# The maxima's rows of two score units added by four 32-row products instead of four 64-row ones

## The chip, the cores and the metric

The kernel runs on one core of one Trainium2 chip, as one launch. The metric is the device time of that launch in microseconds. A core has TensorE for matrix products (PE in the profile, its weight loads PEld), VectorE (DVE), ScalarE (ACT), GpSimd (POOL) and a queue that issues transfers (SP). The engines run side by side and wait for each other only at semaphores. TensorE writes to PSUM, eight banks of 512 float columns on 128 partitions, which VectorE and ScalarE can read.

## The reference, cut to what matters

The program is a chain of four layers on 1024 tokens and 6404 context rows of width 128: a slot attention, a causal attention with experts, a Perceiver cross attention, and a dense mixture of experts. The change lies in the third, which is this, for 16 heads of 64 columns:

```python
x = layer_norm(x, ln1_w, ln1_b)                 # 6404 context rows
lat = layer_norm(latents, ln2_w, ln2_b)         # 1024 latents
lat = lat * (1.0 + scale[:, None, :]) + shift[:, None, :]
q = jnp.einsum('bld,ed->ble', lat, Wq)
kv_in = jnp.concatenate((x, lat), axis=-2)      # 7428 keys
kv = jnp.einsum('bld,ed->ble', kv_in, Wkv)
...
logits = jnp.einsum('bhqd,bhkd->bhqk', q * attn_scale, k * attn_scale)
w = jax.nn.softmax(logits.astype(jnp.float32), axis=-1).astype(logits.dtype)
out = jnp.einsum('bhqk,bhkd->bhqd', w, v)
```

Every query has its own largest logit over 7428 keys, and the softmax subtracts it before the exponential.

## The kernel before

The work is cut into 16 halves `h`: two heads (one on partitions 0 to 63, the other on 64 to 127) and 512 of the 1024 queries. Within a half the keys come in 15 steps `s` of 512 keys, each of four units `i` of 128 keys; the last step (`s = 14`) has the units 56, 57 and 58, the last with four keys only. The names below are those of the code.

A unit (`scores`, L1917 on) makes the scores of 128 keys by 512 queries for both heads, in a slot of two PSUM banks. There are two slots, taken in turn, so a unit waits (`wait_free`) until ScalarE has read the unit two before it. Per head four products of 64 rows add up in one bank: `m = 0` adds the negated maxima, by a matrix with ones in the head's first row (`one_rows`) against `q_shift`, which holds the negated maxima in that row; `m = 1, 2, 3` are the parts of a product in two precisions (`k_high` with `q_high`, `k_low` with `q_high`, `k_high` with `q_low`). The products of the two heads use different rows of the array and run side by side. ScalarE then takes the exponential of both banks in one instruction (L2021) and writes `probs`.

Between these products stand the fills (L1913): plain 64-row products for the maxima of the next half. Each goes to one of three banks (`fill_bank`), VectorE reduces it (L2070), and a fill waits (`peaked`) until all reductions up to that of the third fill before it are done. Every unit of the halves 0 to 14 has one fill per head, placed among its products by `PLACES`; in a step's first unit it stands ahead of them, with place `(0, 0)`. In the last step one more pair of fills stands ahead of the first unit. Half 15 has no fills.

After a step's four units TensorE does, in odd halves, a `produce` (keys and values of the next pair of heads, L1891 and L1897), and then the adds (L1954): eight products of 128 rows by 64 columns that weigh the values with the previous step's `probs`. The order of all this is one list (`perceiver_order`), and every engine walks through it.

The maxima of a half are reduced (L2110) and negated (L2112) into `peak` on VectorE, transposed on TensorE (`shift`, L1962) and copied to `q_shift` by ScalarE. `one_rows` and `peak` are cleared by VectorE in a block of its own ahead of the layer (L1826 on).

Of the kernel before, what the change touches and what calls it, by code (L numbers as in the profile page):

```python
# [4 lines left out]
F32 = mybir.dt.float32  # L5


F32R = mybir.dt.float32r
# [1650 lines left out]

PLACES = ((0, 0), (0, 1), (0, 0), (0, 2))  # L1660


def turns_of(place):

    lanes = [[(head, m) for m in range(4)] for head in range(2)]
    for head in range(2):
        lanes[head].insert(place[head], ("fill", head))
    return [turn for both in zip(*lanes) for turn in both]
# [72 lines left out]
def perceiver_attention(k, A, rows):  # L1741
# [16 lines left out]
    values_of = {e[3:5]: n for e, n in made_values.items()}  # L1758
    scored = {e[1:3]: number[e] for e in entries if e[0] == "scores"}
    fills = []  # L1760
    for e in order:
# [7 lines left out]
    with ExitStack() as ctx:  # L1769
# [5 lines left out]
        q_shift = k.sb("pair_q_shift", [P, HALF], F32R, ctx=ctx)  # L1775
        one_rows = k.sb("pair_one_rows", [P, P], F32R, ctx=ctx)
        probs = k.sb("pair_probs", [P, 2, 4, 2, HALF], ctx=ctx)
        total = k.sb("pair_total", [P, 2, HALF], ctx=ctx)
# [12 lines left out]
        heads = (slice(0, HD1), slice(HD1, P))  # L1791
        peak_columns = peak[:].rearrange("p (n c) -> p n c", c=TQ)[:, 0:HD1 // TQ + 1:HD1 // TQ, :]

        def wait(engine, name, n):
            if n > 0:
                engine.wait_ge(S[name].sem, S[name].at(n))
# [28 lines left out]
        with nc.Block() as block:  # L1825
            @block.vector  # L1826
            def _(v):
                v.memset(one_rows[:].bitcast(F32), 0.0).then_inc(S["cleared"].sem, 1)
                v.memset(peak[:], 0.0).then_inc(S["cleared"].sem, 1)
                wait(v, "cleared", 2)  # L1830
                for row in (0, HD1):
                    v.memset(one_rows[row:row + 1].bitcast(F32), 1.0).then_inc(S["cleared"].sem, 1)
                wait(v, "cleared", 4)

        with nc.Block() as block:
# [21 lines left out]
            def _(pe):  # L1857
# [43 lines left out]
                def fill(f, head):  # L1901
# [8 lines left out]
                    else:  # L1910
# [4 lines left out]
                              stop=True).then_inc(S["filled"].sem, 1)  # L1915

                def scores(e, h, i, f):  # L1917
                    wait_free(e)
                    if i == 0:
                        wait(pe, "qlow", number["queries", h])  # L1920
                        wait(pe, "shifted", number["shift", h])
                    if i % 4 == 0:
                        wait(pe, "low", keys_of[h // 2, i // 4])
                    n = parts_of(i)
                    r, columns = ring_of(h // 2, i // 4), slice(i % 4 * P, i % 4 * P + n)
# [6 lines left out]

                    turns = [(head, m) for m in range(4) for head in range(2)]
                    if f is not None:
                        turns = turns_of(PLACES[i % 4])
                    final = [turn for turn in turns if turn[0] != "fill"][-1]
# [21 lines left out]
                def shift(e, h):  # L1958
                    wait_free(e)
                    wait(pe, "negated", number["peak", h])  # L1960
                    for t in range(TQ):
                        last = pe.transpose(slot(e)[:, 0, t * P:(t + 1) * P], peak[:, t:t + P], k.ident[:])  # L1962
                    last.then_inc(S["made"].sem, 1)
# [94 lines left out]
            def _(v):  # L2058
# [28 lines left out]
                for e in order:  # L2087
# [17 lines left out]
                    elif e[0] == "peak":  # L2105
                        h = e[1]
                        wait(v, "peaked", 2 * fill_number["fill", h, LAST, TQ - 1] + 2)
                        if h:
                            wait_made(v, ("shift", h - 1))
                        v.reduce_max(peak_columns, peaks[:], axis=AX).then_inc(S["largest"].sem, 1)  # L2110
                        wait(v, "largest", h + 1)
                        v.tensor_scalar(peak_columns, peak_columns, -1.0, None, ALU.mult).then_inc(S["negated"].sem, 1)  # L2112
                    elif e[0] == "sum":
# [141 lines left out]
```

## Time and profile before

| | us |
|---|---|
| median of 3 runs | 3549.62 |
| lowest and highest | 3545.74 and 3551.71 |
| the profiled execution's own time | 3550.18 |
| its span in the trace | 3548.5 |

| engine | busy us | share of the span |
|---|---|---|
| PE | 3184.4 | 90% |
| DVE | 2474.4 | 70% |
| POOL | 1872.4 | 53% |
| PEld | 1860.8 | 52% |
| ACT | 1690.0 | 48% |

The span is that of the instructions on the chip, and the execution's own time lies 1.7 us above it. The Perceiver layer takes the part from some 1014 us to 3400 us. An entry of the timeline has the start, the length, the engine and the line, what is written and read, the shape of the tile of weights (`64*128` is 64 rows by 128 columns), the number of instructions merged, and in brackets the idle time before it with its releaser. Matmuls are pipelined: the distance of two starts says how long the first one holds the array, and the length of an entry is longer than that.

### The profile page before, as it was taken

The numbers are of one execution on the slowest core, as the hardware profiler recorded it, in microseconds if no ns is written. First come the engines' busy times: TensorE is split into PE (matmuls) and PEld (weight loads), VectorE is DVE, ScalarE is ACT, GpSimd is POOL, SyncE is SP. The second block draws the span as 40 slices with busy tenths as digits, with TensorE's granted clock in tenths as the row PEclk, the third lists the DMA queues.
The fourth block names the chain that finished last, engine by engine and source line by source line (L and its number), as shares of the span: only waits on it lengthen the run. The fifth ranks groups of instructions, "written<-read, shape, count | busy, mean of one in ns | idle before, by whom it ended". The sixth has DMA issues, their size and how long they took to land. (4 is left out here: it accounts for less than half of the span.)

```text
span 3548.5 us, 51026 instructions
## 1 busy us (share of the span) xinstructions
PE 3184.4 (90%) x18472; PEld 1860.8 (52%) x18472; DVE 2474.4 (70%) x4297; ACT 1690.0 (48%) x2048; POOL 1872.4 (53%) x1158
## 2 busy tenths in 40 slices
PE   5979797586448999999999999999999999999977
PEld 3757575332324555555555555555555555555435
DVE  6979797653258776877777777687777777768431
ACT  5758585243213444454444444445444444444432
POOL 3857575111222655655655565565565566556750
PEclk8989898566679999999999999999999999999988
DMA  1000000000410000000000000000000000000000
GB/s 62 1 1 1 1 1 1 12 1 1 139 21 3 1 1 1 4 1 1 4 1 1 1 4 1 1 4 1 1 4 1 1 1 2 1 1 1 1 26 7
DMA packets 20416, 28.21 MB, mean 8 GB/s; under 512 B 5064, under 2 KB 12368, under 8 KB 20048
## 3 DMA queue, kind: packets, MB, share of 16 engines
q1 hardware_dynamic: 18832, 21.83, 1.9%
q0 software_dynamic: 1344, 3.15, 0.3%
q8 instruction: 154, 2.52, 0.3%
q14 instruction: 86, 0.70, 0.1%
HBM read 21.30 MB, written 3.67 MB: 7 GB/s over the span
## 5 line engine op out<-in xcount | busy, mean ns | idle before, releaser
L2021 ACT ACTIVATE pair_probs<-banks 128x1024 f32<-128x1024 f32 (+1 forms) x944 | 965.7, 1026 | 1035.8 <-PE banks L1931 983.9
L2070 DVE TENSOR_REDUCE pair_peaks<-banks 128x1 f32<-128x512 f32 (+1 forms) x1800 | 1086.4, 666 | 271.3 <-PE banks L1913 257.9
L2163 POOL TENSOR_TENSOR pair_total_pool<-pair_total_pool,pair_probs 128x1536 f32<-128x1536 f32 x208 | 724.5, 3483 | 754.2 <-DVE pair_total L2084 749.0
L1954 PE MATMUL banks<-pair_probs,pair_values 128*64 128x512 f32 (+1 forms) x3776 | 872.9, 600 | 0.0
L1913 PE MATMUL banks<-pair_k_high,pair_q_high 64*128 64x512 f32 (+1 forms) x1920 | 567.3, 442 | 27.3 <-DVE pair_peaks L2063 14.8
L2152 POOL TENSOR_TENSOR pair_total_pool<-pair_total_pool,pair_probs 128x1024 f32<-128x1024 f32 x224 | 536.0, 2393 | 39.1 <-POOL pair_total_pool L2163 21.5
L2084 DVE TENSOR_TENSOR pair_total<-pair_total,pair_probs 128x512 f32<-128x512 f32 (+2 forms) x464 | 458.2, 988 | 94.3 <-ACT pair_probs L2021 69.1
L1954 PEld LDWEIGHTS banks<-pair_probs,pair_values 128*64 128x64 f32 (+1 forms) x3776 | 248.3, 136 | 472.8 <-issue 384.9
L1931 PE MATMUL banks<-pair_q_shift,pair_one_rows 64*128 64x512 f32 (+1 forms) x1888 | 476.1, 396 | 3.1 <-ACT pair_probs L2021 3.1
L1913 PEld LDWEIGHTS banks<-pair_k_high,pair_q_high 64*128 64x128 f32 x1920 | 262.8, 184 | 356.1 <-issue 212.3
L1931 PE MATMUL banks<-pair_q_high,pair_k_high 64*128 64x512 f32 (+1 forms) x1888 | 427.5, 391 | 0.0
L1931 PE MATMUL banks<-pair_q_low,pair_k_high 64*128 64x512 f32 (+1 forms) x1888 | 381.3, 390 | 0.0
L1931 PE MATMUL banks<-pair_q_high,pair_k_low 64*128 64x512 f32 (+1 forms) x1888 | 380.8, 390 | 0.0
L1931 PEld LDWEIGHTS banks<-pair_q_shift,pair_one_rows 64*128 64x128 f32 (+1 forms) x1888 | 243.7, 184 | 34.3 <-ACT pair_probs L2021 11.5
L766 POOL TENSOR_TENSOR value_tile<-context_rows,slot_small 128x128 f32<-128x128 f32 x153 | 198.3, 1296 | 88.4 <-DVE slot_small L638 84.4
L1931 PEld LDWEIGHTS banks<-pair_q_high,pair_k_high 64*128 64x128 f32 (+1 forms) x1888 | 221.8, 183 | 33.7
L2098 DVE TENSOR_TENSOR pair_k_low<-banks,pair_k_high 128x512 fp32r<-128x512 f32 (+1 forms) x120 | 80.9, 674 | 220.5 <-ACT pair_k_high L2031 219.3
L543 ACT ACTIVATE slot_probs<-banks,slot_small 128x1024 f32<-128x1024 f32 x153 | 171.1, 1118 | 81.9 <-DVE slot_small L645 81.9
L1931 PEld LDWEIGHTS banks<-pair_q_high,pair_k_low 64*128 64x128 f32 (+1 forms) x1888 | 184.4, 183 | 40.0 <-issue 0.8
L1931 PEld LDWEIGHTS banks<-pair_q_low,pair_k_high 64*128 64x128 f32 (+1 forms) x1888 | 184.9, 183 | 38.3
L643 DVE TENSOR_REDUCE slot_small<-banks 128x1 f32<-128x1024 f32 x153 | 187.0, 1222 | 19.1 <-PE banks L439 7.7
L651 DVE TENSOR_TENSOR slot_probs_low<-slot_probs,slot_probs_high 128x1024 fp32r<-128x1024 f32 x153 | 193.0, 1261 | 6.3 <-ACT slot_probs_high L547 5.5
(325 smaller groups left out, 3776.3 us busy)
## 6 DMA issues: line engine op xcount, KB each, us to landing
expert_w<-in_fc SPq DMA_DIRECT2D x32, 256.0 KB, 3.6
context_rows<-in_ctx SPq DMA_DIRECT2D x10, 320.0 KB, 6.7
dense_w<-in_We SPq DMA_DIRECT2D x2, 1024.0 KB
experts_in<-expert_zeros SPq DMA_DIRECT2D x1, 1024.0 KB, 3.8
expert_b<-in_fc_b SPq DMA_DIRECT2D x2, 512.0 KB, 5.0
expert_rows<-experts_in SPq DMA_DIRECT2D x16, 64.0 KB, 1.9
experts_out<-expert_result POOLq DMA_DIRECT2D x4, 256.0 KB, 3.7
row_parameters<-in_rows SPq DMA_DIRECT2D x1, 896.0 KB, 8.7
```

Of the source, the lines that this page charges most:

```text
L543: done("expd", act.activation(probs[0:n, r, :], flat(scores[r][0:n]), ACT.Exp, bias=small[0:n, r, 1:2], scale=SLOT_SCALE, accum_out=small[ ...
L643: done("largest", v.reduce_max(small[0:n, r, 0:1], flat(scores[r][0:n]), axis=AX))
L651: done("subbed", v.tensor_tensor(probs_low[0:n, r, 0:TOKENS], probs[0:n, r, 0:TOKENS], probs_high[0:n, r, 0:TOKENS].bitcast(F32), ALU.subt ...
L766: done("weighed", pool.tensor_tensor(value[0:n, r, :], rows[0:n, i, :], small[0:n, r, 3:4].to_broadcast([n, D]), ALU.mult))
L1913: pe.matmul(bank[:, 0:width(b)], q_high[h % 2][heads[head], t * P:(t + 1) * P], k_high[heads[head], ring_of(h // 2, b), 0:width(b)], start ...
L1931: return pe.matmul(slot(e)[0:n, head, :], left, right, start=m == 0, stop=m == 3)
L1954: last = pe.matmul(out[heads[head], :], values[0:n, ring_of(h // 2, i // 4), i % 4, heads[head]], probs_of(h, i)[0:n, head, :], start=i == ...
L2021: act.activation(probs_of(h, i)[0:n], slot(e)[0:n], ACT.Exp, scale=1.0 / 8.0).then_inc(S["expd"].sem, 1)
L2070: v.reduce_max(peaks[:, head, t, b:b + 1], fill_bank(f, head)[:, 0:width(b)], axis=AX).then_inc(S["peaked"].sem, 1)
L2084: v.tensor_tensor(total[0:n, both], total[0:n, both], probs_of(h, i)[0:n, both], ALU.add).then_inc(S["summed"].sem, 1)
L2152: pool.tensor_tensor(pooled[:, 1:3], pooled[:, 1:3], probs_of(h, 4 * s + 3), ALU.add).then_inc(S["pooled"].sem, 1)
L2163: pool.tensor_tensor(pooled[:], pooled[:], three, ALU.add).then_inc(S["pooled"].sem, 1)
```

## The change

In a step, the first two units are a pair if both stand next to each other in the list of slots, in one step, and no `output` or `denominators` stands just before them. That gives 210 pairs: 15 in half 0 and 13 in each of the others.

Where a pair starts, TensorE waits for both slots and then issues four products of 32 rows (`share_shift`), one for each head of each unit, into four banks. `q_shift` now holds the negated maxima in rows 0, 32, 64 and 96, and `lane_rows` has ones in these rows. The two units then make their products `m = 1, 2, 3` alone. All other units keep their own `m = 0` with `one_rows`. The maxima are first reduced to a tile of their own (`largest`) and then negated into two places of `peak`, by two instructions. The number of TensorE's products stays the same.

```diff
 PLACES = ((0, 0), (0, 1), (0, 0), (0, 2))
+LANE = 32
+FIRST_OF_TWO = (0,)
-def turns_of(place):
-    lanes = [[(head, m) for m in range(4)] for head in range(2)]
+def turns_of(products, place):
+    lanes = [[(head, m) for m in products] for head in range(2)]
     for head in range(2):
-        lanes[head].insert(place[head], ("fill", head))
+        if place is not None:
+            lanes[head].insert(place[head], ("fill", head))
...
+    partner = {}
+    for n, e in enumerate(entries[:-1]):
+        if e[0] == "scores" and e[2] % 4 in FIRST_OF_TWO and entries[n + 1][0:2] == e[0:2] and e[2] < TILES \
+                and entries[n + 1][2] // 4 == e[2] // 4 and entries[n - 1][0] not in ("output", "denominators"):
+            partner[e] = entries[n + 1]
+    second = set(partner.values())
...
-                wait(v, "cleared", 2)
+                v.memset(lane_rows[:].bitcast(F32), 0.0).then_inc(S["cleared"].sem, 1)
+                wait(v, "cleared", 3)
                 for row in (0, HD1):
                     v.memset(one_rows[row:row + 1].bitcast(F32), 1.0).then_inc(S["cleared"].sem, 1)
-                wait(v, "cleared", 4)
+                for row in range(0, P, LANE):
+                    v.memset(lane_rows[row:row + 1].bitcast(F32), 1.0).then_inc(S["cleared"].sem, 1)
+                wait(v, "cleared", 9)
...
+                def share_shift(units):
+                    for u, unit in enumerate(units):
+                        n = parts_of(unit[2])
+                        for head in range(2):
+                            lane = slice(head * HD1 + u * LANE, head * HD1 + (u + 1) * LANE)
+                            pe.matmul(slot(unit)[0:n, head, :], lane_rows[lane, 0:n], q_shift[lane, :], start=True, stop=False)
+
                 def scores(e, h, i, f):
-                    wait_free(e)
+                    if e not in second:
+                        wait_free(e)
...
+                    if e in partner:
+                        wait_free(partner[e])
+                        share_shift((e, partner[e]))
...
-                    turns = [(head, m) for m in range(4) for head in range(2)]
-                    if f is not None:
-                        turns = turns_of(PLACES[i % 4])
+                    products = range(1, 4) if e in partner or e in second else range(4)
+                    turns = turns_of(products, None if f is None else PLACES[i % 4])
...
-                    wait(pe, "negated", number["peak", h])
+                    wait(pe, "negated", 2 * number["peak", h])
...
-                        v.reduce_max(peak_columns, peaks[:], axis=AX).then_inc(S["largest"].sem, 1)
+                        v.reduce_max(largest[:], peaks[:], axis=AX).then_inc(S["largest"].sem, 1)
                         wait(v, "largest", h + 1)
-                        v.tensor_scalar(peak_columns, peak_columns, -1.0, None, ALU.mult).then_inc(S["negated"].sem, 1)
+                        for columns in peak_columns:
+                            v.tensor_scalar(columns, largest[:], -1.0, None, ALU.mult).then_inc(S["negated"].sem, 1)
```

How the instructions move is shown by TensorE's list at a step's start, from a unit's last product to the third unit. The shapes in these lists are those of the result. In the kernel before, L1954 is an add, L1913 a fill, and L1931 the products of a unit, `pair_q_shift` being `m = 0`:

```order
3909 L1954 MATMUL banks<-pair_probs,pair_values 64x512 x8
3910 L1913 MATMUL banks<-pair_k_high,pair_q_high 128x512 x2
3911 L1931 MATMUL banks<-pair_q_shift,pair_one_rows 128x512 x2
3912 L1931 MATMUL banks<-pair_q_high,pair_k_high 128x512 x2
3913 L1931 MATMUL banks<-pair_q_high,pair_k_low 128x512 x2
3914 L1931 MATMUL banks<-pair_q_low,pair_k_high 128x512 x2
3915 L1913 MATMUL banks<-pair_k_high,pair_q_high 128x512
3916 L1931 MATMUL banks<-pair_q_shift,pair_one_rows 128x512 x2
3917 L1913 MATMUL banks<-pair_k_high,pair_q_high 128x512
3918 L1931 MATMUL banks<-pair_q_high,pair_k_high 128x512 x2
```

The same place in the changed kernel, where the lines are L1979 for the add, L1928 for the fill, L1957 for a unit's products, and L1937 for the shared ones:

```order
3851 L1979 MATMUL banks<-pair_probs,pair_values 64x512 x8
3852 L1937 MATMUL banks<-pair_q_shift,pair_lane_rows 128x512 x4
3853 L1928 MATMUL banks<-pair_k_high,pair_q_high 128x512 x2
3854 L1957 MATMUL banks<-pair_q_high,pair_k_high 128x512 x2
3855 L1957 MATMUL banks<-pair_q_high,pair_k_low 128x512 x2
3856 L1957 MATMUL banks<-pair_q_low,pair_k_high 128x512 x2
3857 L1928 MATMUL banks<-pair_k_high,pair_q_high 128x512
3858 L1957 MATMUL banks<-pair_q_high,pair_k_high 128x512 x2
3859 L1928 MATMUL banks<-pair_k_high,pair_q_high 128x512
3860 L1957 MATMUL banks<-pair_q_high,pair_k_low 128x512 x2
```

The four shared products stand between the adds and the first unit's fills. The first unit has as many turns ahead of its last product as before, and the second unit has one turn fewer.

In a half's last step TensorE's list reads so in the kernel before, with the extra pair of fills and the first unit's pair in one row:

```order
2932 L1954 MATMUL banks<-pair_probs,pair_values 64x512 x8
2933 L1913 MATMUL banks<-pair_k_high,pair_q_high 128x260 x4
2934 L1931 MATMUL banks<-pair_q_shift,pair_one_rows 128x512 x2
2935 L1931 MATMUL banks<-pair_q_high,pair_k_high 128x512 x2
2936 L1931 MATMUL banks<-pair_q_high,pair_k_low 128x512 x2
```

And so in the changed one, at the same kind of place:

```order
4997 L1979 MATMUL banks<-pair_probs,pair_values 64x512 x8
4998 L1928 MATMUL banks<-pair_k_high,pair_q_high 128x260 x2
4999 L1937 MATMUL banks<-pair_q_shift,pair_lane_rows 128x512 x4
5000 L1928 MATMUL banks<-pair_k_high,pair_q_high 128x260 x2
5001 L1957 MATMUL banks<-pair_q_high,pair_k_high 128x512 x2
5002 L1957 MATMUL banks<-pair_q_high,pair_k_low 128x512 x2
```

Here the shared products come between the two pairs of fills. 15 of the 210 pairs are of this kind, and 13, those of half 15, have no fills at all.

## Rows read from the trace of the kernel before

**Rows 1.** The page: busy time by engine, and the granted clock in 40 slices.
```profile
PE 3184.4 (90%) x18472; PEld 1860.8 (52%) x18472; DVE 2474.4 (70%) x4297; ACT 1690.0 (48%) x2048; POOL 1872.4 (53%) x1158
...
PEclk8989898566679999999999999999999999999988
```
**Rows 2.** Stretch of the layer: window, length, busy of PE, PEld, DVE, ACT, POOL, PEclk.
```profile
1500.00:2000.00 500.00, 496.44 (x3092) 271.59 (x3090) 367.40 (x555) 241.92 (x273) 290.11 (x108) 1.00 0.01 2
```
**Rows 3.** Timeline of PE in one step of half 2: start, length, instruction.
```profile
1489.34 0.50 PE L1913 MATMUL banks<-pair_k_high,pair_q_high 64*128 64x512 f32 x2
1489.67 0.39 PE L1931 MATMUL banks<-pair_q_shift,pair_one_rows 64*128 64x512 f32 x2
1489.90 0.39 PE L1931 MATMUL banks<-pair_q_high,pair_k_high 64*128 64x512 f32 x2
...
1490.37 0.39 PE L1931 MATMUL banks<-pair_q_low,pair_k_high 64*128 64x512 f32 x2
...
1491.52 0.41 PE L1931 MATMUL banks<-pair_q_low,pair_k_high 64*128 64x512 f32 x2
1491.88 0.50 PE L1913 MATMUL banks<-pair_k_high,pair_q_high 64*128 64x512 f32 x2
```
**Rows 4.** Timeline of PEld in the same step, where its third unit starts.
```profile
1491.88 0.19 PEld L1913 LDWEIGHTS banks<-pair_k_high,pair_q_high 64*128 64x128 f32 x2 [0.38 <-ACT pair_probs L2021]
1491.99 0.19 PEld L1931 LDWEIGHTS banks<-pair_q_shift,pair_one_rows 64*128 64x128 f32 x2
```
**Rows 5.** Timeline of ACT in that step, its first and second exponential.
```profile
1490.80 1.03 ACT L2021 ACTIVATE pair_probs<-banks 128x1024 f32<-128x1024 f32 x1 [3.91 <-PE banks L1931]
...
1491.96 1.03 ACT L2021 ACTIVATE pair_probs<-banks 128x1024 f32<-128x1024 f32 x1
```
**Rows 6.** Timeline of DVE in that step, its first and third reduction.
```profile
1489.87 0.69 DVE L2070 TENSOR_REDUCE pair_peaks<-banks 128x1 f32<-128x512 f32 x1 [1.69 <-PE banks L1913]
...
1491.08 0.68 DVE L2070 TENSOR_REDUCE pair_peaks<-banks 128x1 f32<-128x512 f32 x1
```
**Rows 7.** Waits of PEld, 1100 to 3400 us: total, times, longest.
```profile
PEld banks L1913 <- ACT pair_probs L2021: 111.3, 359, 0.5
```
**Rows 8.** Timeline of PE: from 64-row products to 128-row ones.
```profile
1494.08 0.39 PE L1931 MATMUL banks<-pair_q_low,pair_k_high 64*128 64x512 f32 x2
1494.40 1.08 PE L1954 MATMUL banks<-pair_probs,pair_values 128*64 128x512 f32 x4
```
**Rows 9.** Timelines of PEld and PE: adds of 128 rows, then of 4.
```profile
1247.68 0.17 PEld L1954 LDWEIGHTS banks<-pair_probs,pair_values 128*64 128x64 f32 x2 [0.26 <-issue]
1248.11 0.17 PEld L1954 LDWEIGHTS banks<-pair_probs,pair_values 128*64 128x64 f32 x2 [0.26 <-issue]
...
1248.57 1.17 PE L1954 MATMUL banks<-pair_probs,pair_values 128*64 128x512 f32 x3
...
1249.09 1.07 PE L1954 MATMUL banks<-pair_probs,pair_values 4*64 4x512 f32 x4
```
**Rows 10.** Timelines in the causal layer: four 32-column tiles, two 25-row tiles.
```profile
703.61 0.20 PEld L1013 LDWEIGHTS banks<-causal_probs,values_by_head 128*32 128x32 f32 x4 [0.44 <-issue]
...
700.24 0.79 PE L994 MATMUL banks<-keys,queries 25*128 25x512 f32 x2 [0.69 <-ACT causal_probs L1103]
```
**Rows 11.** Timeline of PE in a step of half 15, without fills.
```profile
3388.59 0.50 PE L1931 MATMUL banks<-pair_q_shift,pair_one_rows 64*128 64x512 f32 x2
...
3390.91 0.50 PE L1931 MATMUL banks<-pair_q_shift,pair_one_rows 64*128 64x512 f32 x2 [0.20 <-ACT pair_probs L2021]
```
**Rows 12.** Timelines of PE and DVE in the last step of half 2.
```profile
1523.94 0.50 PE L1913 MATMUL banks<-pair_k_high,pair_q_high 64*128 64x260 f32 x3
1524.84 0.39 PE L1913 MATMUL banks<-pair_k_high,pair_q_high 64*128 64x260 f32 x1 [0.40 <-DVE pair_peaks L2070]
...
1525.18 0.52 PE L1931 MATMUL banks<-pair_q_high,pair_k_high 64*128 64x512 f32 x2
...
1524.36 0.43 DVE L2070 TENSOR_REDUCE pair_peaks<-banks 128x1 f32<-128x260 f32 x1 [1.58 <-PE banks L1913]
```
**Rows 13.** Timelines of DVE: the rows of ones, and the negation in half 0.
```profile
1015.32 0.41 DVE L1832 MEMSET pair_one_rows<- 1x128 f32 x2
...
1104.91 0.17 DVE L2112 TENSOR_SCALAR pair_peak_columns<-pair_peak_columns 128x8 f32<-128x8 f32 x1
```

More of the change, by code:

```diff
@@ L1776, in perceiver_attention @@
         one_rows = k.sb("pair_one_rows", [P, P], F32R, ctx=ctx)
+        lane_rows = k.sb("pair_lane_rows", [P, P], F32R, ctx=ctx)
+        largest = k.sb("pair_largest", [P, 2, TQ], ctx=ctx)
         probs = k.sb("pair_probs", [P, 2, 4, 2, HALF], ctx=ctx)
@@ L1791, in perceiver_attention @@
         heads = (slice(0, HD1), slice(HD1, P))
-        peak_columns = peak[:].rearrange("p (n c) -> p n c", c=TQ)[:, 0:HD1 // TQ + 1:HD1 // TQ, :]
+        peak_columns = [peak[:].rearrange("p (n c) -> p n c", c=TQ)[:, lane // TQ:(lane + HD1) // TQ + 1:HD1 // TQ, :]
+                        for lane in (0, LANE)]
         def wait(engine, name, n):
```

## Prediction

> **What bounds the kernel now.** I read the page's busy times and clock first, then the windows of the layer, then the timelines of one step on PE, PEld, ACT and DVE, and last what ended the idle times. TensorE is busy 90% of the span, and its granted clock is at the full level of 2.4 GHz from the middle of the slices on [rows 1]; within the layer it is busy 496.44 of 500 us [rows 2]. By that share each product saved would count. The reader is to distrust this: an entry of a matmul is longer than the distance to the next one, so a stall of a tenth of a microsecond is covered by it.
>
> One step shows the stall. The pair of fills starts at 1489.34 and the first product pair at 1489.67, 0.33 later; the next follows at 1489.90, 0.23 later [rows 3]. So a pair of 64-row products holds the array for 0.23, and the first after a pause costs 0.10 to 0.11 more, which is its weights' load: at 1491.88 and 1491.99 the loads of two pairs start 0.11 apart [rows 4]. The first unit's last pair starts at 1490.37 [rows 3]; its exponential runs from 1490.80 for 1.03 us, to 1491.83 [rows 5]; the third unit, which needs the first one's slot, starts at 1491.88 [rows 3], with ACT named as the releaser and its loads idle for 0.38 [rows 4]. The second unit's last pair had started at 1491.52 [rows 3], so TensorE would have been ready at 1491.75: it waits 0.13 there. The chain from the step's start to its third unit is thus first unit, exponential, third unit: 1.03 + 0.43 + 1.03 + 0.05 = 2.54 us. The second unit lies beside it. The same wait stands in the whole layer: 359 idle times of the fills' loads end by ACT, 0.31 us each [rows 7], where halves 0 to 14 have 225 steps. Half 15, without fills, waits there too, 0.20 us of PE's own idle time [rows 11].
>
> A second chain runs close beside it. VectorE starts the first fill's reduction at 1489.87 and the third at 1491.08, which ends at 1491.76 [rows 6]: three reductions back to back, 0.60 apart. The second fill of the third unit goes to a bank which the third of these reductions must have left. With a hand-over of 0.05 it could go at 1491.81, and goes at 1491.88 [rows 3]. So this chain has 0.07 us to spare. The hand-over from VectorE is seen in the last step: a reduction from 1524.36 for 0.43 us, to 1524.79, and the waiting fill at 1524.84 [rows 12].
>
> **The change part by part.** I count from a step's start, t = 0.
>
> The four shared products take the array once, 0.23, in place of two pairs, 2 x 0.23. The second of these was the second unit's, which lies beside the chain through the exponential. What it frees, 210 x 0.23 = 48 us, comes ahead of a stall that nothing shortens: the exponential of the first unit still follows that unit's last product, with just as many turns ahead of it as before. The gain on the path is zero.
>
> What is added is on the path. The array goes from 32-row products back to 64-row ones right behind the shared four. The rows show what a change of the rows costs. From a 64-row pair to 128-row adds it takes 0.32 instead of 0.23 (1494.08 to 1494.40) [rows 8]. Between adds, which follow each other at 0.43 (1247.68, 1248.11), the change from 128 rows to 4 takes 0.52 (1248.57 to 1249.09) [rows 9]. Each is 0.09 over the usual distance, and then the new weights' load is exposed as after a pause, another 0.11 for 128 columns. The change from the adds into the first scores was there before, so only one is new. I put the first unit's fills at 0.11 + 0.23 + 0.09 = 0.43 instead of 0, its `m = 1` at 0.43 + 0.34 = 0.77 instead of 0.57, and its last product 0.20 later than now. No row has 32 rows followed by 64, so the bounds are 0 (the loads are pulled ahead as between 64-row pairs) and 0.20; I take 0.20, since both row-count changes that the trace has cost it.
>
> The Trainium skill says in "TensorEngine Tiling (Array Packing)", Key Properties, that a change of the tiling mode drains TensorE, while a change of the tile within a mode doesn't. By this rule 64 to 32 to 64 rows is two changes and each waits for the array; rows 8 and 9 agree in size, 0.09 us. Without such a drain the fills would come at 0.34 and the first unit's last product not later at all.
>
> By the chain over ScalarE alone the third unit comes 0.20 later. By the chain over VectorE it is worse: the first fill, and with it the first reduction, moves by 0.43, while the reductions stay 0.60 apart. The third ends at 2.42 + 0.43 = 2.85, and the third unit's second fill can go at 2.90 instead of 2.54: 0.36 later. That is the larger one and sets the end. TensorE issues in order, so behind this fill stand the third unit's own products, its exponential, the fourth unit and the adds. Afterwards nothing gives the time back: fourth unit and adds run at TensorE's pace.
>
> Of the 210 pairs 13 are in half 15, with no fills: 13 x 0.20 = 2.6 us. 15 are in last steps, where an extra pair of 260-column fills comes first. There the first unit's second fill already waits for VectorE until 1524.84, 0.90 after the step's start, and its `m = 1` starts at 1525.18, or 1.24 [rows 12]. The shared four now fit into that wait: extra fills 0.11 + 0.11, drain 0.09, the four and the way back 0.43, so 0.74, still under 0.90; then `m = 1` comes at 0.90 + 0.11 + 0.11 = 1.12. That is 0.1 earlier: 15 x 0.1 = 1.5 us gained. The other 182 give 182 x 0.36 = 65.5 us.
>
> Small edits: one more clearing of a tile and four more rows of ones, in a block that the layer waits for. Two rows of ones take 0.41 with the second 0.24 behind the first [rows 13], so four add 1.0, and the tile some 0.15: 1.1 us once. The second negation is exposed in half 0 alone, where TensorE waits for it: 0.17 to 0.25, taken as 0.2 [rows 13]. In other halves adds stand between. The wait for the second slot at a pair's start costs nothing as long as the four adds, 8 x 0.43 = 3.4 us, cover the last exponential (0.43 + 1.03 + 0.05 behind the fourth unit's last product). In odd halves the copies of keys and values are in that slot; they have the same 3.4 us. Without this cover each such step would lose what is missing. For the wait's own instruction I take nothing; TensorE's queue reads it while the adds run.
>
> Sum: 65.5 + 2.6 - 1.5 + 1.1 + 0.2 = 67.9 us. Against the profiled execution, 3550.18, that is 3618.1. The median of the runs is 0.6 lower, which gives 3617.5; I say 3617.
>
> **The rivals.**
>
> *The way back to 64 rows is free.* Then the fills come at 0.34, `m = 1` where it is now, and ScalarE's chain is unchanged. VectorE's chain still shifts: 2.42 + 0.34 + 0.05 = 2.81 against 2.54, 0.27 for 182 pairs, or 49 us; with 1.3 for the small edits and 1 or 2 off in last steps, 3599. For it: pairs in different halves of the array overlap their loads already. Against it: rows 8 and 9.
>
> *Only ScalarE's chain counts.* The reductions turn out to have more room, say because they could start closer together once fills wait for them. Then 182 x 0.20 + 2.6 - 1.5 + 1.3 = 38.8, so 3588. Against it: three reductions run back to back now.
>
> *The four products don't run wholly side by side.* At the worst they go two by two, 0.23 more: the fills at 0.66, VectorE's chain at 0.59, ScalarE's at 0.43: 182 x 0.59 + 13 x 0.43 + 1 + 1.3 = 115, so 3665. The rows have four loads merged in 0.20 us for 32-column tiles, and two 25-row tiles at once [rows 10], but never four row tiles; the lower bound is nothing, and I take the four as one.
>
> The Trainium skill gives in "TensorE: Matmul & The Clock Gate", Measured speedup vs the span model, 3.07 times for four tiles of 32 rows by 512 columns. Four over 3.07 is 1.30 of one product, an estimate of 0.07 us more each; the sum would be 182 x 0.43 + 13 x 0.27 and the same small terms, some 82 us, so 3631. No row here shows it.
>
> *Faster: the turn saved counts.* If TensorE and not the exponential set the start of the third unit, and changes of rows were free, 210 x 0.23 = 48 us would go: 3501. It decides from the point where the exponential of the first unit ends before the second unit's last turn is over; now it ends 0.08 after it. For it speak only the busy shares of rows 1 and 2; against it rows 4, 7 and 11.
>
> *No change.* The way back is free and VectorE keeps up after all: 3551.
>
> **How the numbers follow.** Forecast 0.58, free way back 0.12, ScalarE alone 0.08, four products wider 0.13 (spread between 3625 and 3665), no change 0.04, faster 0.05. The range from 3582 to 3645 holds the first three and about half of the fourth, 0.84 in all; inside the forecast a drain of 0.05 to 0.12 and a hand-over of 0.05 to 0.15 give 3609 to 3640. About 0.2%, 7 us, is what a measurement of this kernel can tell from no change. Faster 0.05, within it 0.04, slower 0.91.
>
> **What would show it.** In the new timeline the distance from the shared four to the fills should be 0.43, from a step's first product to its third unit 2.90 for the second fill and some 2.74 for the first, with VectorE as the releaser of the second; a step should be 0.36 longer in halves 1 to 14, and 0.20 in half 15. VectorE's first reduction should start 0.96 after the step's start instead of 0.53. The distance 0.34 would show the free way back; two loads of the shared four 0.2 apart would show that they don't overlap; and idle loads of the third unit named after ACT alone would show that VectorE's chain doesn't count. It is wrong altogether if the third unit starts less than 2.5 us after the step.

## The result, and the profile after

The changed kernel takes 3610.2 us (median of 4 runs, 3607.47 to 3612.32), the kernel before 3549.05 (4 runs, 3545.74 to 3551.71). The ratio is 1.0172, with a 95% interval of 1.0155 to 1.019: slower by 61 us, where 67.9 were forecast (3617, range 3582 to 3645). A turn, here as in the prediction, is one pair of products side by side, 0.23 us of the array. The profiled execution has 3610.98 us and a span of 3609.3.

The page again shows a TensorE that is 90% busy, and not where the loss is. Both its busy time and the span grew, by 48 and 61 us:

```profile
PE 3232.2 (90%) x18472; PEld 1944.7 (54%) x18472; DVE 2459.3 (68%) x4318; ACT 1687.6 (47%) x2048; POOL 1869.0 (52%) x1158
...
PEclk8989898666779999999999999999999999999988
```

The timeline of PE for a full step of half 2 and the start of the next (start, length, instruction) answers to [rows 3]:

```profile
1512.04 0.50 PE L1937 MATMUL banks<-pair_q_shift,pair_lane_rows 32*128 32x512 f32 x4
...
1521.02 0.50 PE L1937 MATMUL banks<-pair_q_shift,pair_lane_rows 32*128 32x512 f32 x4
1521.45 0.50 PE L1928 MATMUL banks<-pair_k_high,pair_q_high 64*128 64x512 f32 x2
1521.78 0.39 PE L1957 MATMUL banks<-pair_q_high,pair_k_high 64*128 64x512 f32 x2
...
1522.23 0.39 PE L1957 MATMUL banks<-pair_q_low,pair_k_high 64*128 64x512 f32 x2
...
1523.74 0.68 PE L1928 MATMUL banks<-pair_k_high,pair_q_high 64*128 64x512 f32 x2
```

From the shared four to the fills it is 0.43, as forecast, and to `m = 1` 0.76 (forecast 0.77). The first unit's last product is 1.21 after the step's start, where it was 1.03. The third unit's first fill is 2.72 after it; before it was 2.54. The entry of the pair of fills at 1523.74 is 0.68 long instead of 0.50: its two halves don't start together any more. A step takes 1521.02 - 1512.04 = 8.98. In the kernel before the same stretch took 8.65:

```profile
1480.69 0.50 PE L1913 MATMUL banks<-pair_k_high,pair_q_high 64*128 64x512 f32 x2
```

(the next step there starts at 1489.34 [rows 3]).

The timelines of ACT and DVE in that step, first exponential, then first and third reduction:

```profile
1522.66 1.03 ACT L2046 ACTIVATE pair_probs<-banks 128x1024 f32<-128x1024 f32 x1 [4.10 <-PE banks L1957]
```
```profile
1521.98 0.69 DVE L2095 TENSOR_REDUCE pair_peaks<-banks 128x1 f32<-128x512 f32 x1 [2.17 <-PE banks L1928]
...
1523.18 0.68 DVE L2095 TENSOR_REDUCE pair_peaks<-banks 128x1 f32<-128x512 f32 x1
```

The first reduction starts 0.96 after the step's start (0.53 before [rows 6]) and the third ends at 1523.86. The loads of PEld around the third unit show when the second fill goes:

```profile
1523.74 0.36 PEld L1928 LDWEIGHTS banks<-pair_k_high,pair_q_high 64*128 64x128 f32 x2 [0.49 <-ACT pair_probs L2046]
1523.92 0.18 PEld L1957 LDWEIGHTS banks<-pair_q_shift,pair_one_rows 64*128 64x128 f32 x1
```

One load is 0.18; the pair's entry of 0.36 means that the second starts 0.18 after the first, at 1523.92: 2.90 after the step's start, 0.06 after the third reduction. That is the forecast number. The row's bracket names ACT, the releaser of the entry's first load; that the second one waits for VectorE is seen only from its start and the reduction's end. The 0.18 between the two loads is also just the length of one, so this step alone doesn't exclude that the second simply follows the first. The whole trace does: over the 181 steps that are like this one (regular steps, below), the second fill's load starts 0.053 to 0.054 after the end of the third reduction in nine tenths of them, while its distance to the first load varies from 0.15 to 0.18. In the kernel before it starts 0.12 to 0.14 after that reduction and 0.003 after the first load.

Half 15 has no fills, and a last step has an extra pair. Their PE rows answer to [rows 11, 12]:

```profile
3456.40 0.51 PE L1937 MATMUL banks<-pair_q_shift,pair_lane_rows 32*128 32x512 f32 x4
...
3458.91 0.50 PE L1957 MATMUL banks<-pair_q_shift,pair_one_rows 64*128 64x512 f32 x2 [0.42 <-ACT pair_probs L2046]
```
```profile
1538.96 0.39 PE L1928 MATMUL banks<-pair_k_high,pair_q_high 64*128 64x260 f32 x2
1539.28 0.51 PE L1937 MATMUL banks<-pair_q_shift,pair_lane_rows 32*128 32x512 f32 x4
1539.72 0.53 PE L1928 MATMUL banks<-pair_k_high,pair_q_high 64*128 64x260 f32 x2
1539.95 0.53 PE L1957 MATMUL banks<-pair_q_high,pair_k_high 64*128 64x512 f32 x2
```

In half 15 the third unit starts 2.51 after the step's start, 2.32 before [rows 11]. In the last step the first unit's `m = 1` comes 0.99 after the start instead of 1.24 [rows 12]: the shared four fit into the wait for VectorE.

To sum up the layer I took the time between the exponentials of the last units of successive steps, in the traces of both kernels. The 181 steps with a pair and fills (without last steps and the very first step; called regular steps below) are longer by 0.33 each, 59.9 us together. The 13 of half 15: 0.21 each, 2.7. The 15 last steps: shorter by 0.22, -3.3. The steps without a pair: -2.1, of which -2.4 in step 1 of the odd halves. There TensorE waits for GpSimd's sum, and a later arrival waits less. The very first step: -0.8. That is 56.4 us between the first and the last exponential, and 4.3 come before it. The waits of PE for that sum, before and then after (total, times, longest):

```profile
PE banks L1969 <- POOL pair_total_pool L2135: 5.5, 8, 0.7
```
```profile
PE banks L1994 <- POOL pair_total_pool L2161: 3.0, 8, 0.6
```

The eight waits, one in each odd half, are 2.5 us shorter in all.

### The profile page after: what moved, and what is told of

Read it like the earlier page. It is cut to its first block and busy times, and to the rows that moved or that the text cites. A ratio compares the mean times of both kernels' runs of the same rounds, so it can differ in the third digit from the quotient of the medians.

```text
span 3609.3 us, 50934 instructions
## 1 busy us (share of the span) xinstructions
PE 3232.2 (90%) x18472; PEld 1944.7 (54%) x18472; DVE 2459.3 (68%) x4318; ACT 1687.6 (47%) x2048; POOL 1869.0 (52%) x1158
## 5 line engine op out<-in xcount | busy, mean ns | idle before, releaser
L1979 PE MATMUL banks<-pair_probs,pair_values 128*64 128x512 f32 (+1 forms) x3776 | 873.0, 600 | 0.0
L1928 PE MATMUL banks<-pair_k_high,pair_q_high 64*128 64x512 f32 (+1 forms) x1920 | 618.2, 453 | 35.2 <-DVE pair_peaks L2088 14.2
L1979 PEld LDWEIGHTS banks<-pair_probs,pair_values 128*64 128x64 f32 (+1 forms) x3776 | 248.5, 136 | 472.1 <-issue 384.9
L1957 PE MATMUL banks<-pair_q_high,pair_k_high 64*128 64x512 f32 (+1 forms) x1888 | 464.6, 392 | 0.0
L1957 PE MATMUL banks<-pair_q_high,pair_k_low 64*128 64x512 f32 (+1 forms) x1888 | 457.9, 390 | 0.0
L1957 PE MATMUL banks<-pair_q_low,pair_k_high 64*128 64x512 f32 (+1 forms) x1888 | 457.5, 390 | 0.0
L1928 PEld LDWEIGHTS banks<-pair_k_high,pair_q_high 64*128 64x128 f32 x1920 | 292.7, 185 | 252.2 <-ACT pair_probs L2046 115.0
L1957 PEld LDWEIGHTS banks<-pair_q_low,pair_k_high 64*128 64x128 f32 (+1 forms) x1888 | 262.5, 183 | 16.5 <-issue 0.3
L1957 PEld LDWEIGHTS banks<-pair_q_high,pair_k_high 64*128 64x128 f32 (+1 forms) x1888 | 260.2, 183 | 15.6 <-issue 3.2
L1957 PEld LDWEIGHTS banks<-pair_q_high,pair_k_low 64*128 64x128 f32 (+1 forms) x1888 | 259.1, 183 | 15.5
L1957 PE MATMUL banks<-pair_q_shift,pair_one_rows 64*128 64x512 f32 (+1 forms) x1048 | 262.0, 394 | 5.9 <-ACT pair_probs L2046 5.9
L547 ACT ACTIVATE slot_probs_high<-slot_probs 128x1024 fp32r<-128x1024 f32 x153 | 162.3, 1061 | 5.4 <-PE banks L451 0.6
```

What stands on the lines that cost most here:

```text
L1928: pe.matmul(bank[:, 0:width(b)], q_high[h % 2][heads[head], t * P:(t + 1) * P], k_high[heads[head], ring_of(h // 2, b), 0:width(b)], start ...
L1957: return pe.matmul(slot(e)[0:n, head, :], left, right, start=m == 0, stop=m == 3)
L1979: last = pe.matmul(out[heads[head], :], values[0:n, ring_of(h // 2, i // 4), i % 4, heads[head]], probs_of(h, i)[0:n, head, :], start=i == ...
```

## The experiments

All are run beside the kernel before on the same chip, whose time is given with them. "Per step" is the mean change of the 181 regular steps, taken as above.

**e1_first_alone.** The row change without the saved turn.

```diff
-                    if e not in second:
-                        wait_free(e)
+                    wait_free(e)
...
                     if e in partner:
-                        wait_free(partner[e])
-                        share_shift((e, partner[e]))
+                        share_shift((e,))
...
-                    products = range(1, 4) if e in partner or e in second else range(4)
+                    products = range(1, 4) if e in partner else range(4)
```

> The changed kernel, but only the first unit's m = 0 goes through 32-row products (two of them, rows 0 and 64); the second unit keeps its own 64-row pair, so no turn is saved. Theory (the cost is the change of rows on the path of the first unit, the saved turn lies beside the stall and is worth nothing): the same as the changed kernel, 3610 within 5 us, and 0.33 us per step over before as there; the third unit's fills still start at 2.7 and 2.9 us after the step's start. Rival (the saved turns count, 210 x 0.23 us): 3658. Rival (four tiles hold the array longer than two): shorter than the changed kernel, by 0.05 us or more from the 32-row products to the fills.

Measured: 3616.87 us against 3553.18, ratio 1.0177 (1.0159 to 1.0194), which is the changed kernel's ratio; 0.345 per step. PE's timeline:

```profile
1503.68 0.50 PE L1937 MATMUL banks<-pair_q_shift,pair_lane_rows 32*128 32x512 f32 x2
1504.11 0.50 PE L1928 MATMUL banks<-pair_k_high,pair_q_high 64*128 64x512 f32 x2
...
1506.43 0.65 PE L1928 MATMUL banks<-pair_k_high,pair_q_high 64*128 64x512 f32 x2
```

The time itself lies 6.7 us above the changed kernel's 3610.2, a little more than the 5 allowed, but the kernel before was 4.1 us higher in these runs too; the ratios are the same. Giving the saved turn back costs nothing, or 0.01 per step. And two 32-row products take the same 0.43 to the fills as four: the four run side by side. Both rivals fall.

**e2_second_left_out.** The saved turn without the row change. On the changed kernel's source, without `share_shift`:

```diff
-                    if e in partner:
-                        wait_free(partner[e])
-                        share_shift((e, partner[e]))
...
-                    products = range(1, 4) if e in partner or e in second else range(4)
+                    products = range(1, 4) if e in second else range(4)
```

The first product that is left then starts the sum in the bank.

> The changed kernel without the shared products: the first unit of a pair has its own 64-row m = 0 as before, the second unit's m = 0 is left out (its maxima are not subtracted). This is the saved turn without the change of rows. Theory: worth nothing, since the second unit lies beside the first one's exponential: 3549 to 3552 us, steps as long as before, the third unit's wait longer by 0.23. Rival (TensorE is the bound, a turn is worth 0.23): 3549 - 48 = 3501.

Measured: 3551.68 us (10 runs) against 3553.18 (13), ratio 1.0 (0.999 to 1.0009); -0.015 per step. A step's start and its third unit on PE, and the third unit's loads:

```profile
1488.22 0.50 PE L1928 MATMUL banks<-pair_k_high,pair_q_high 64*128 64x512 f32 x2
...
1490.77 0.50 PE L1928 MATMUL banks<-pair_k_high,pair_q_high 64*128 64x512 f32 x2 [0.20 <-ACT pair_probs L2042]
```
```profile
1490.76 0.19 PEld L1928 LDWEIGHTS banks<-pair_k_high,pair_q_high 64*128 64x128 f32 x2 [0.63 <-ACT pair_probs L2042]
```

The third unit stands where it stood, 2.55 after the step's start, and its loads idle for 0.63 instead of 0.38 [rows 4]. 210 turns of 0.23 us, 48 us of TensorE's work, are gone and the time is the same. The rival of 3501 falls.

**e3_first_left_out.** A turn taken from the path of the first exponential. As e2, with the first unit's `m = 0` left out:

```diff
-                    products = range(1, 4) if e in partner or e in second else range(4)
+                    products = range(1, 4) if e in partner else range(4)
```

> As the last one, but the first unit's m = 0 of each pair is left out instead (its maxima are not subtracted), and the second unit has its own. Now a turn goes from the path of the exponential, while the first fills stay where they are. Theory of two chains: the exponential's chain gets shorter by 0.23 but VectorE's third reduction holds the third unit's second fill at 2.47 instead of 2.54, so 0.07 per step: 182 x 0.07 + 13 x 0.23 + 15 x 0.2 = 19 us, 3530, with VectorE as the releaser of the second fill. Rival (only ScalarE's chain counts): 210 x 0.23 = 48, 3501.

Measured: 3532.76 us against 3553.18, ratio 0.9945 (0.9929 to 0.9962). Per step -0.09 (expected -0.07), in half 15 -0.23, in last steps -0.23. The third unit on PEld in a step that starts at 1493.21, and VectorE's third reduction:

```profile
1495.53 0.34 PEld L1928 LDWEIGHTS banks<-pair_k_high,pair_q_high 64*128 64x128 f32 x2 [0.27 <-ACT pair_probs L2042]
```
```profile
1494.95 0.68 DVE L2091 TENSOR_REDUCE pair_peaks<-banks 128x1 f32<-128x512 f32 x1
```

The first fill goes at 2.32, the second 0.34 - 0.18 = 0.16 later, at 2.48, behind the reduction that ends at 2.42. Of 0.23 us that the exponential's chain gives back, 0.09 arrive; where there are no fills, all do. In nine tenths of the regular steps the second fill's load starts 0.052 to 0.054 after the third reduction, as in the changed kernel. VectorE's chain is the second bound, just under the first.

**e4_late_fill.** The changed kernel, with VectorE's chain out of the third unit's way:

```diff
-PLACES = ((0, 0), (0, 1), (0, 0), (0, 2))
+PLACES = ((0, 0), (0, 1), (0, 2), (0, 2))
```

> The changed kernel with the third unit's second fill two turns later (place 2 instead of 0 in PLACES), so that it does not wait for VectorE's third reduction. Theory: what is left is ScalarE's chain, 0.20 to 0.21 per step instead of 0.33, as in half 15: 3610 - 182 x 0.13 = 3586. Rival (VectorE's chain does not count, the 0.33 is all row changes): 3610. If VectorE is short of time later in the step, between the two.

Measured: 3585.57 us against 3553.18, ratio 1.0098 (1.0081 to 1.0115); 0.19 per step instead of 0.33. PE's timeline:

```profile
1496.68 0.50 PE L1937 MATMUL banks<-pair_q_shift,pair_lane_rows 32*128 32x512 f32 x4
...
1499.41 0.50 PE L1928 MATMUL banks<-pair_k_high,pair_q_high 64*128 64x512 f32 x1
1499.41 0.73 PE L1957 MATMUL banks<-pair_q_shift,pair_one_rows 64*128 64x512 f32 x2
```

Both halves of the array start at 2.73 now. This parts the loss in two: 0.19 to 0.20 by the row change through ScalarE, and 0.14 more by the late fills through VectorE. The kernel before was not run with this place, but the steps without a pair can stand in for that: in the 30 of them, of which 28 have fills, e4 and the changed kernel differ by 0.2 us in all. The move by itself is worth nothing there.

**e5_fills_first.** The changed kernel with the first unit's fills ahead of the shared four, so that VectorE starts early:

```diff
                     if e in partner:
                         wait_free(partner[e])
+                        if f is not None:
+                            for head in range(2):
+                                fill(f, head)
                         share_shift((e, partner[e]))
```

> The changed kernel with the first unit's fills ahead of the shared four instead of behind them, so the array goes 64 to 32 to 64 rows and VectorE's reductions start as early as before. Theory: two new changes of rows instead of one, so the first unit's m = 1 at 0.11 + 0.23 + 0.09 + 0.11 + 0.23 + 0.09 = 0.86 instead of 0.57, and the third unit 0.29 later, released by ScalarE alone; in last steps the shared four now stand behind the fill that waits for VectorE, so 0.4 lost instead of 0.22 gained. 182 x 0.29 + 15 x 0.4 + 2.7 - 2 = some 60 us over before: 3605 to 3615. Rival (the cost of the changed kernel is ScalarE's alone, one change of rows 0.33): 0.66 per step, 3670. Rival (changes of rows are free in themselves, the cost came from the late fills): 3550.

Measured: 3628.28 us against 3549.33, ratio 1.0219 (1.0203 to 1.0235). Per step 0.40, not 0.29; in last steps 0.41. This expectation missed by 0.11. PE's timeline:

```profile
1505.40 0.50 PE L1928 MATMUL banks<-pair_k_high,pair_q_high 64*128 64x512 f32 x2
1505.83 0.51 PE L1937 MATMUL banks<-pair_q_shift,pair_lane_rows 32*128 32x512 f32 x4
1506.27 0.51 PE L1960 MATMUL banks<-pair_q_high,pair_k_high 64*128 64x512 f32 x2
1506.61 0.40 PE L1960 MATMUL banks<-pair_q_high,pair_k_low 64*128 64x512 f32 x2
...
1508.37 0.50 PE L1928 MATMUL banks<-pair_k_high,pair_q_high 64*128 64x512 f32 x2 [0.19 <-ACT pair_probs L2049]
```

`m = 1` starts at 0.87, as worked out. But `m = 2` follows 0.34 later and not 0.23, since behind each change of rows the load is exposed; I had counted it for two of three. So a change of rows costs 0.20 each time, and two cost 0.40. The rest of the theory fits: the third unit starts 2.97 after the step's start, both fills at once and with ACT as the releaser, so the chain over ScalarE is the longer one and VectorE's early start gains nothing. Both rivals fall, 0.66 per step and no loss.

**e7_fills_ahead.** The kernel before, with the stall used. The third unit's fills don't need its slot, so they go ahead of the wait:

```diff
                 def scores(e, h, i, f):
+                    early = f is not None and i % 4 == 2
+                    if early:
+                        for head in range(2):
+                            fill(f, head)
                     wait_free(e)
...
-                    if f is not None:
+                    if f is not None and not early:
                         turns = turns_of(PLACES[i % 4])
```

> The kernel before (no shared products) with one move: the third unit's fills are issued ahead of the wait for its slot, since they need a bank of their own and not the slot. They fill the stall behind the first unit's exponential. Theory: the fills go at 2.41 and 2.47 (VectorE's third reduction ends at 2.42), the third unit's own products at 2.64 and 2.8 instead of 2.88, and the fourth unit waits for the second exponential until 3.70 instead of starting at 3.83: 0.13 us per step in 225 steps, 29 us, so 3520 (3512 to 3530). Rival (the stall moves whole to the fourth unit or to the adds): 3550. Rival (fills ahead collide with VectorE): slower than before.

Measured: 3544.19 us (11 runs) against 3549.33 (21), ratio 0.9988 (0.9979 to 0.9997); -0.03 per step, -0.24 in last steps. The expectation, 3520 and 0.13 per step, missed. PE's timeline of a step that starts at 1486.07, and the fourth unit's load:

```profile
1488.47 0.57 PE L1913 MATMUL banks<-pair_k_high,pair_q_high 64*128 64x512 f32 x2
1488.69 0.58 PE L1935 MATMUL banks<-pair_q_shift,pair_one_rows 64*128 64x512 f32 x2
...
1489.76 0.49 PE L1913 MATMUL banks<-pair_k_high,pair_q_high 64*128 64x512 f32 x1
```
```profile
1489.76 0.18 PEld L1913 LDWEIGHTS banks<-pair_k_high,pair_q_high 64*128 64x128 f32 x1 [0.22 <-ACT pair_probs L2025]
```

The fills go at 2.40, the unit's own products at 2.62, and the fourth unit at 3.69, all as expected. But the fourth unit now stands behind a wait, and a product behind a wait pays for its load: 0.11 of the 0.13 is lost again, which I had left out. The stall has moved by one unit, and the rival of 3550 was nearer to the result than the theory.

**e8_ahead_and_last.** The changed kernel with the move of e7 (its edit isn't shown again), and with the shared four in last steps alone:

```diff
-        if e[0] == "scores" and e[2] % 4 in FIRST_OF_TWO and entries[n + 1][0:2] == e[0:2] and e[2] < TILES \
+        if e[0] == "scores" and e[2] == 4 * LAST and entries[n + 1][0:2] == e[0:2] and e[2] < TILES \
```

> The move of e7 together with the shared four in the last step of each half alone, 15 or 16 pairs, where they run inside a fill's wait for VectorE. Theory: 0.22 us in each of 15 last steps as in the changed kernel, 3.3 us, less 0.2 lost in the half without fills and 1.3 us for clearing lane_rows: 1 to 2 us below e7, within the measurement's noise, with the last steps 0.2 us shorter in the timeline. Rival (the move of e7 takes the wait away that hid them): equal to e7 or above it by 3 us.

Measured: 3541.69 us (11 runs) against 3549.33 (21), ratio 0.998 (0.9971 to 0.9989). Last steps are 0.48 shorter than before, twice e7's 0.24. So the two gains add, and in this one place the shared four are worth a turn, as the expectation had it. The difference to e7 as a whole, 2.5 us, is within the scatter of the runs; only the steps in the trace show it.

**e9_two_units_ahead.** e8, with the fourth unit's fills ahead of its wait too, and half 15 left as before:

```diff
-        if e[0] == "scores" and e[2] == 4 * LAST and entries[n + 1][0:2] == e[0:2] and e[2] < TILES \
+        if e[0] == "scores" and e[2] == 4 * LAST and e[1] + 1 < HALVES and entries[n + 1][0:2] == e[0:2] and e[2] < TILES \
...
-                    early = f is not None and i % 4 == 2
+                    early = f is not None and i % 4 in (2, 3)
```

> As e8, with the fourth unit's fills issued ahead of the wait for its slot too, and no shared products in the half without fills. In e7 the fourth unit starts 3.69 us after the step, held by the second exponential, and its first products pay their weights' load behind that wait. Theory: the fills run in that wait, at 3.55 and 3.67 (VectorE's fifth reduction ends at 3.62), the unit's own products at 3.78 and 4.01, so its last product comes 0.0 to 0.05 earlier and the load is hidden: 0.02 to 0.1 us per step in 225 steps, 3520 to 3540, below e8's 3542. Rival (VectorE's reductions, eight per step at 0.60, now set the pace and hold the fill beyond 3.69): e8's time or up to 10 us above it.

Measured: 3534.59 us (5 runs) against 3551.8 (9), ratio 0.9952 (0.9938 to 0.9965); -0.07 per step, -0.47 in last steps. PE's timeline of a step that starts at 1489.53:

```profile
1491.94 0.56 PE L1928 MATMUL banks<-pair_k_high,pair_q_high 64*128 64x512 f32 x2
1492.17 0.57 PE L1961 MATMUL banks<-pair_q_shift,pair_one_rows 64*128 64x512 f32 x2
...
1492.88 0.56 PE L1961 MATMUL banks<-pair_q_low,pair_k_high 64*128 64x512 f32 x2
1493.10 0.59 PE L1928 MATMUL banks<-pair_k_high,pair_q_high 64*128 64x512 f32 x2
1493.33 0.60 PE L1961 MATMUL banks<-pair_q_shift,pair_one_rows 64*128 64x512 f32 x2
```

From 1491.94 on the pairs of the two units follow at 0.23 each with no gap between the units. This version is faster than both kernels, by 0.5% over the one before, and its ratio lies below e8's, as expected; VectorE's reductions don't hold the fills, and that rival falls.

## Why the prediction was right

*Where the turn saved goes.* It was put at nothing, since the second unit lies beside the first one's exponential. Shown by e2 (removing the turn alone: ratio 1.0) and e1 (giving it back: no change).

*The way back to 64 rows.* It was put at 0.20 us on the path, from two other changes of rows in [rows 8, 9]. Shown: 0.43 from the shared four to the fills, 0.21 per step in half 15, 0.19 per step in e4, and twice that in e5. The "free way back" falls. The loads of the fills behind the shared four show the exposed part. PEld idles for 0.24 before them, and they start only with their own products:

```profile
1521.44 0.19 PEld L1928 LDWEIGHTS banks<-pair_k_high,pair_q_high 64*128 64x128 f32 x2 [0.24 <-issue]
```

The Trainium skill says in "TensorEngine Tiling (Array Packing)", Key Properties, that a change of the tiling mode drains TensorE. The trace agrees: 0.43 from the shared four to the fills, 0.09 more than the 0.34 that a pair with an exposed load takes.

*VectorE's chain.* The third unit's second fill was put at 2.90 and goes at 2.90. By the prediction's own sign, idle loads of the third unit named after ACT alone, the rival would have been taken for true: ACT is the only name in that row. The sign was badly chosen, since the row names the releaser of the first of two loads. That VectorE's chain is the cause is shown by e4, where nothing changes but that fill's place and 0.14 per step goes away, and by e3, where it keeps 0.14 of 0.23 from arriving. "Only ScalarE's chain" falls.

*The four side by side.* e1 has the same 0.43 with two. The prediction's estimate of 0.07 more, from the figure for four tiles in the Trainium skill ("TensorE: Matmul & The Clock Gate", Measured speedup vs the span model), doesn't hold here: the 0.43 from the shared four to the fills leaves no room for it.

*The sizes.* The step that was mis-sized is "the other 182 give 182 x 0.36": they give 0.33 each, 60 us instead of 65.5. The 0.36 is there at the third unit's second fill. Behind it only one half of the array is late, and it makes up 0.03 in the products of the third and fourth unit, ahead of the adds. In the step from 1512.04:

```profile
1516.95 0.55 PE L1957 MATMUL banks<-pair_q_low,pair_k_high 64*128 64x512 f32 x2
1517.43 3.65 PE L1979 MATMUL banks<-pair_probs,pair_values 128*64 128x512 f32 x16
```

The late half's last product starts 0.55 - 0.39 = 0.16 after the other's, 5.07 after the step's start, and the adds 5.39; before it was 4.74 and 5.06 [rows 8], so both are 0.33 later. Last steps were put at -0.1 and gave -0.22. There I compared the time of the later half of the array after the change (1.12) with that of the earlier half before it (1.24); half for half the chain gets shorter by a whole turn. The 2.4 us that the odd halves get back at their wait for GpSimd were not foreseen, nor the 0.8 of the very first step. The clearing of `lane_rows` was put at 1.1 us:

```profile
1015.65 0.17 DVE L1840 MEMSET pair_one_rows<- 128x128 f32 x1 [0.59 <-PEq L1639]
...
1016.67 0.90 DVE L1847 MEMSET pair_lane_rows<- 1x128 f32 x4
```

From the first clearing to the layer's first transfer it is 2.39 us where it was 1.27 (by SP's timeline, at 1018.04), so 1.1. The other 3.2 us ahead of the first exponential are only partly accounted for: 0.3 is the first pair itself, 0.7 is there before the layer begins, in code that is the same; 2.1 come between the first transfer and the copy of the first `q_shift`, a stretch in which e2 and e4, with the same code there, are within 0.3 us of the kernel before, e1, e3, e5 and e9 show the 2 us too, and e8, also with the same code, is 1.4 us shorter. It differs between traces of the same code and I count it as scatter; its cause is not known. In it lies the second negation, put at 0.2: from the first negation to the copy of `q_shift` it is 1.51 where it was 1.44, so 0.07.

The account by steps adds up to the measured 61 us. That the forecast misses it by no more than 7 us is in part luck: some 3 us of gain that were not foreseen and some 3 us ahead of the layer's first exponential, scatter for the most part, cancel.

## What to carry to other kernels

An engine that is 99% busy in a window can still not be the bound: look at what ended the wait of the one instruction that stands still in each round, and count only work that lies ahead of it. Work beside the stall is free, in both directions, and the way to gain is to move work into it, as e9 does, not to remove work from it. A mode that packs small products better is to be charged with entering and leaving: here each change of the rows costs 0.20 us against a turn of 0.23. And what is put in front of a producer delays its consumer's whole chain: the fills were 0.43 late, and an engine with 0.07 us to spare became the bound.

## What the runs showed of the hardware

Four 32-row products in different rows of the array and different banks take as long as two (0.43 to the next change in both, e1), in the float32r type used here. A change of rows from 32 to 64 or back costs 0.09 of drain and 0.11 of exposed load each time: in e5 the starts are 0.43 apart from 64 to 32 rows, 0.44 from 32 to 64, then 0.34 within 64 rows, where pairs otherwise follow at 0.23.

The two halves of the array can run 0.18 us apart without loss of pace. Behind the third unit's staggered fills at 1523.74 the changed kernel's PE timeline goes on so, each entry holding both halves:

```profile
1524.09 0.57 PE L1957 MATMUL banks<-pair_q_shift,pair_one_rows 64*128 64x512 f32 x2
1524.32 0.57 PE L1957 MATMUL banks<-pair_q_high,pair_k_high 64*128 64x512 f32 x2
```

The distance is the usual 0.23, and the length 0.57 instead of 0.39 is the stagger.
